# A GRU with a ternary FFN on one core: order of the first loads, the casts and warm-up products at the kernel's start

## The reference

```python
def cell(h, x):                       # 32 times, one after the other
    gi = x @ W_ih + b_ih              # [128, 256] @ [256, 768]
    gh = h @ W_hh + b_hh
    r = sigmoid(i_r + h_r)
    z = sigmoid(i_z + h_z)
    n = tanh(i_n + r * h_n)
    return (1.0 - z) * n + z * h
...
gate, up = split(hs @ ternary(w_gate_up).T)
out = x + rms_norm(silu(gate) * up) @ ternary(w_proj).T
```

## Time and profile before

| | us |
|---|---|
| median of 3 runs | 345.35 (344.94 to 345.5) |
| the profiled execution | 345.16 |
| its span, first to last instruction | 343.4 |
| TensorE busy | 338.2 (98%) |
| VectorE, ScalarE, GpSimd busy | 233.1 (68%), 224.9 (66%), 184.1 (54%) |

### The profile page before, as it was taken

How to read it: one execution, slowest core, us unless ns; L and a number is a source line. 1 busy time by engine, 2 the same in 40 slices (tenths; PEclk the granted TensorE clock), 3 DMA queues, 4 the chain that set the end, 5 groups by cost and what they waited for, 6 DMA issues and landing times.

```text
span 343.4 us, 5618 instructions
## 1 busy us (share of the span) xinstructions
PE 338.2 (98%) x2048; PEld 294.4 (86%) x2053; DVE 233.1 (68%) x462; ACT 224.9 (66%) x442; POOL 184.1 (54%) x156
## 2 busy tenths in 40 slices
PE   8999999999999999999999999999999999999996
PEld 4989988888988889888888889888888888888895
DVE  7588787999576556754678554775658555665866
ACT  6778888787755757555766666566565655756662
POOL 2316571465825536255454447454462555799694
PEclk9999999999999999999999999999999999999999
DMA  7995000054001000130001000010000100010101
GB/s 241 299 402 224 2 0 2 0 186 183 1 2 62 2 0 0 71 115 2 0 0 63 0 2 1 1 63 0 2 0 15 48 1 2 0 64 1 59 4 61
DMA packets 7891, 18.72 MB, mean 55 GB/s; under 512 B 564, under 2 KB 4788, under 8 KB 7352
## 3 DMA queue, kind: packets, MB, share of 16 engines
q1 hardware_dynamic: 7176, 17.97, 14.1%
q10 hardware_dynamic: 688, 0.39, 0.4%
HBM read 14.17 MB, written 4.19 MB: 53 GB/s over the span
## 4 chain that ended last, share of the span: by engine, by line
PE 90%; DVE 5%; issue 2%; ACT 1%; DVEq 0%
PE ps_ffn L1126 29%; PE ps_out L1164 16%; PE ps_rz L1028 6%; PE ps_rz L1033 6%; PE ps_rz L1029 6%; PE ps_n L1028 3%; PE ps_n L1033 3%; PE ps_n L1029 3%; PE ps_rz L1126 2%; PE ps_t L1119 1%; PE ps_ffn L1291 1%; PE ps_n L1077 1%; PE ps_ffn L1028 1%; PE ps_ffn L1033 1%; PE ps_ffn L1029 1%
## 5 line engine op out<-in xcount | busy, mean ns | idle before, releaser
L359 POOL TENSOR_TENSOR hid_lo<-work,hid_hi 128x512 fp32r<-128x512 f32 x62 | 81.6, 1316 | 103.5 <-ACT hid_hi L457 99.5
L1126 PE MATMUL ps_ffn<-st_hi,wguT 128*128 128x512 f32 x236 | 93.8, 397 | 0.1
L1126 PE MATMUL ps_ffn<-st_lo,wguT 128*128 128x512 f32 x236 | 92.6, 393 | 0.0
L366 POOL TENSOR_TENSOR sq_sum<-sq_sum,work 128x512 f32<-128x512 f32 x55 | 73.2, 1331 | 1.7 <-ACT work L471 0.6
L748 DVE TENSOR_TENSOR work<-work,ps_ffn 128x512 f32<-128x512 f32 x55 | 37.6, 683 | 31.4 <-ACT work L453 31.3
L457 ACT CAST hid_hi<-work 128x512 fp32r<-128x512 f32 x63 | 38.8, 616 | 23.4 <-DVE work L758 23.4
L1126 PEld LDWEIGHTS ps_ffn<-st_hi,wguT 128*128 128x128 f32 x236 | 44.4, 188 | 8.3 <-DVE work L748 0.7
L1126 PEld LDWEIGHTS ps_ffn<-st_lo,wguT 128*128 128x128 f32 x236 | 44.5, 189 | 7.3
L758 DVE TENSOR_TENSOR work<-work,ps_ffn 128x512 f32<-128x512 f32 x63 | 43.2, 686 | 4.7 <-PE ps_ffn L1126 2.8
L1164 PEld LDWEIGHTS ps_out<-wpT,hid_hi 128*128 128x128 f32 x240 | 35.8, 189 | 3.7
L1164 PE MATMUL ps_out<-wpT,hid_lo 128*128 128x256 f32 x240 | 38.8, 284 | 0.0
(11 more groups left out here) (232 smaller groups left out, 713.7 us busy)
## 6 DMA issues: line engine op xcount, KB each, us to landing
out_dram<-o_st SPq DMA_DIRECT2D x7, 512.0 KB, 2.8
xT_all<-in_x_dram SPq DMA_DIRECT2D x1, 3072.0 KB, 16.4
x_ring<-in_x_dram SPq DMA_DIRECT2D x1, 3072.0 KB, 11.2
x_ring<-in_L_ffn_w_gate_up_dram SPq DMA_DIRECT2D x4, 512.0 KB, 9.5
x_ring<-in_L_ffn_w_proj_dram SPq DMA_DIRECT2D x2, 512.0 KB, 11.7
x_ring<-in_x_dram SPq DMA_DIRECT2D x1, 1024.0 KB, 6.0
work<-in_L_cond_W_ih_dram SPq DMA_DIRECT2D x3, 256.0 KB, 4.5
work<-in_L_cond_W_hh_dram SPq DMA_DIRECT2D x3, 256.0 KB, 4.8
```

The source lines that it names most:

```text
L359: nc.gpsimd.tensor_tensor(hid_lo[:, j % RING], hid[:, j % 2], f32(hid_hi[:, j % RING]), ALU.subtract).then_inc(hid_lo_ok, 1)
L366: nc.gpsimd.tensor_tensor(sq_sum[:], sq_sum[:], hid_sq[:, j % 2], ALU.add).then_inc(sq_added, 1)
L1126: mm = pe.matmul(bank, w, group_state(part, G, k), start=(k == 0 and i == 0), stop=(k == KD - 1 and i == 1))
```

## The change

SyncE's first load is W_ih's reset piece, the transposed state cT is second; the two bias rows are issued by ScalarE behind x's step 0. ScalarE casts W_ih's reset piece before the RZ columns of the biases. GpSimd, not VectorE, makes the state's low part. VectorE splits the RZ columns after wi_lo(0). TensorE runs eight warm-up products, seeds the n bank inside first_input(0) ahead of the wi_lo products, and adds the RZ bias row inside first_state(0) ahead of the wh_lo products.

```diff
--- before.py
+++ after.py
@@ -260,12 +260,12 @@
                 for to, w, landed in ((wi, w_ih, ld_wi), (wh, w_hh, ld_wh)):
                     sp.dma_start(to[:, :, GATES[i]],
                                  w.rearrange("(k p) n -> p k n", p=P)[:, :, GATES[i]]).then_inc(landed[i], 16)
+                    if i == 0 and to is wi:
+                        sp.dma_start(cT[:], cond_t.rearrange("(k p) b -> p k b", p=P)).then_inc(ld_cT, 16)
 
             def load_inputs(first, last, landed):
                 sp.dma_start(xT_all[:, :, first:last, :], xt[:, :, first:last, :]).then_inc(landed, 16)
 
-            for i, b in enumerate((b_ih, b_hh)):
-                sp.dma_start(b_rows[:, i * G3:(i + 1) * G3], b.partition_broadcast(2)).then_inc(ld_b, 16)
             for i in range(3):
                 load_gate(i)
             load_inputs(1, 2, ld_x1)
@@ -323,6 +323,8 @@
                                         ALU.subtract).then_inc(x_lo_early, 1)
 
             input_lo(0)
+            pool.wait_ge(h_hi, 1)
+            nc.gpsimd.tensor_tensor(state(st_lo, -1), cT[:], f32(state(st_hi, -1)), ALU.subtract).then_inc(c_lo, 1)
             pool.wait_ge(wh_hi_ok, 3)
             nc.gpsimd.tensor_tensor(wh_lo[:, :, GATES[2]], wh[:, :, GATES[2]], f32(wh_hi[:, :, GATES[2]]),
                                     ALU.subtract).then_inc(wh_z_ok, 1)
@@ -540,16 +542,17 @@
 
             xt = x_t.rearrange("(k p) t b -> p k t b", p=P)
             act.dma_start(xT_all[:, :, 0:1, :], xt[:, :, 0:1, :]).then_inc(ld_x0, 16)
-            act.dma_start(cT[:], cond_t.rearrange("(k p) b -> p k b", p=P)).then_inc(ld_cT, 16)
+            for i, b in enumerate((b_ih, b_hh)):
+                act.dma_start(b_rows[:, i * G3:(i + 1) * G3], b.partition_broadcast(2)).then_inc(ld_b, 16)
             act.wait_ge(consts, 1)
             nc.scalar.activation(table[:], ones[:], ACT.Sigmoid)
             act.wait_ge(ld_x0, 16)
             input_hi(0)
             act.wait_ge(ld_b, 32)
             nc.scalar.copy(both_n(b_hi), both_n(b_all)).then_inc(b_hi_ok, 1)
+            w_ih_hi(0)
             act.wait_ge(b_sum_ok, 1)
             nc.scalar.copy(b_hi[:, RZ], b_all[:, RZ]).then_inc(b_hi_ok, 1)
-            w_ih_hi(0)
             act.wait_ge(ld_cT, 16)
             nc.scalar.copy(state(st_hi, -1), cT[:]).then_inc(h_hi, 1)
             w_hh_hi(0)
@@ -864,10 +867,6 @@
             dve.wait_ge(b_hi_ok, 1)
             nc.vector.scalar_tensor_tensor(out=both_n(b_split[0:2, :]), in0=both_n(f32(b_hi)), scalar=ident[0:2, 1:2],
                                            in1=both_n(b_all), op0=ALU.mult, op1=ALU.subtract).then_inc(b_split_ok, 1)
-            dve.wait_ge(b_hi_ok, 2)
-            nc.vector.scalar_tensor_tensor(out=b_split[0:2, RZ], in0=f32(b_hi[:, RZ]), scalar=ident[0:2, 1:2],
-                                           in1=b_all[:, RZ], op0=ALU.mult, op1=ALU.subtract).then_inc(b_split_ok, 1)
-
             def w_ih_lo(i):
                 dve.wait_ge(wi_hi_ok, i + 1)
                 cols = GATES[i]
@@ -881,8 +880,9 @@
                                         ALU.subtract).then_inc(wh_ok, 1)
 
             w_ih_lo(0)
-            dve.wait_ge(h_hi, 1)
-            nc.vector.tensor_tensor(state(st_lo, -1), cT[:], f32(state(st_hi, -1)), ALU.subtract).then_inc(c_lo, 1)
+            dve.wait_ge(b_hi_ok, 2)
+            nc.vector.scalar_tensor_tensor(out=b_split[0:2, RZ], in0=f32(b_hi[:, RZ]), scalar=ident[0:2, 1:2],
+                                           in1=b_all[:, RZ], op0=ALU.mult, op1=ALU.subtract).then_inc(b_split_ok, 1)
             w_hh_lo(0)
             w_ih_lo(1)
             w_hh_lo(1)
@@ -1301,6 +1301,9 @@
                     for k in range(KD):
                         pe.matmul(dst, part[:, 0, k, :], wi_hi[:, k, cols],
                                   start=i == 0 and k == 0 and part is xT_hi, stop=False, skip_group_check=True)
+                if i == 0:
+                    pe.wait_ge(b_split_ok, 1)
+                    seed_n(0)
                 pe.wait_ge(wi_ok, i + 1)
                 for k in range(KD):
                     pe.matmul(dst, xT_hi[:, 0, k, :], wi_lo[:, k, cols], start=False, stop=False,
@@ -1316,6 +1319,9 @@
                     for k in range(KD):
                         pe.matmul(dst, part[:, k, :], wh_hi[:, k, cols], start=False, stop=False,
                                   skip_group_check=True)
+                if i == 0:
+                    pe.wait_ge(b_split_ok, 2)
+                    bias_rows(ps_rz[:], RZ, False)
                 if i == 1:
                     seed_rz(1)
                 if i < 2:
@@ -1331,13 +1337,10 @@
                 mm.then_inc(summed, 1)
 
             pe.wait_ge(warm_ok, 1)
-            busy(10)
+            busy(8)
             pe.wait_ge(consts, 5)
             first_input(0, ps_rz[:, 0:D])
-            pe.wait_ge(b_split_ok, 2)
-            bias_rows(ps_rz[:], RZ, False)
             first_state(0, ps_rz[:, 0:D], r_sum)
-            seed_n(0)
             first_input(1, ps_n[:, 0:D])
             first_state(1, ps_n[:, D:2 * D], n_sum)
             pe.wait_ge(r_ok, 1)
```

## The result

The changed kernel takes 347.23 us (median of 5 runs, 346.64 to 347.96) against 345.35; the ratio is 1.0053, with a 95% interval of 1.0033 to 1.0074. It is 1.9 us slower, where 0.5 faster was forecast. The profiled execution took 347.96, with a span of 345.8.

The account below looks back on a forecast made before the run. TensorE, busy 90% of the span, was taken as the bound. Between z's gain of 0.6 and the state's cast's 0.55, 0.5 was taken: 344.66 from the profiled 345.16, 344.85 on the median; forecast 344.8, range 344.1 to 345.7.

Parts of the forecast that it names:

- (a): Early loads: W_ih's reset half issued 0.71 earlier, landing at 4.35 for 5.14; biases at 3.6, at worst 3.87.
- S: Start of ScalarE's cast of W_ih's reset half, wi_hi(0): 4.35, at worst 4.4 by the biases.
- (b): ScalarE's early casts: wi_hi(0) starts at 4.35; wh_hi(0) starts at 5.9 and ends at 6.5, against 6.84.
- (c): VectorE and GpSimd: the low state on GpSimd collides with VectorE's work; 0.25 charged, bounds 0 and 0.6.
- (d): TensorE's start: products begin 0.8 earlier, 0.4 gained if the clock rises at 6.65; reset sum 7.75 for 8.19.
- the clock rises later: Rival on TensorE's start: each microsecond more at 1.2 GHz costs half a microsecond; 346.5 if near 10; chance 0.07.
- (e): Late next: ScalarE's q_abs(0), awaiting the gate-up load at 12.15, lets the state's cast come 0.55 earlier; 0.5 taken.
- it doesn't do what it says: Rival on the early loads: W_ih's half lands no earlier than 5.14, TensorE only idles, 345.35; chance 0.07.

Follow-up runs that it names:

- e10: The kernel before without the work on the split biases (bias rows added as zeros): 345.71 us, ratio 1.0009.
- e8: The kernel before with the biases on ScalarE's queue behind x and the state first on SyncE, W_ih's reset half second: 347.41 us, ratio 1.0057.
- e7: The kernel before with one load moved, W_ih's reset half ahead of the two bias rows on SyncE: 347.52 us, ratio 1.0059.
- e3: The kernel before with the new order of loads alone, ten warm-ups: 347.84 us, ratio 1.0071.
- e9: The changed kernel (eight warm-ups, its loads) without the work on the split biases, bias rows added as zeros: 344.82 us, ratio 0.9984.
- e1: The changed kernel with ten warm-up products instead of eight: 346.72 us, ratio 1.0041.
- e6: The changed kernel with ten warm-ups and the state's low part back on VectorE: 346.24 us, ratio 1.0030.
- e12: The changed kernel with the loads of before, ten warm-ups and the state's low part on VectorE: 345.34 us, ratio 1.0002.
- e2: The kernel before with eight warm-up products instead of ten, nothing else changed: 345.56 us, ratio 1.0014.
- e4: The changed kernel with the load order of before, eight warm-ups: 346.78 us, ratio 1.0039.
- e5: The kernel before with one edit, GpSimd making the state's low part: 345.53 us, ratio 1.0006.
- e13: The kernel before with x first on SyncE, W_ih's reset half second, state third, biases alone on ScalarE's queue, ten warm-ups: 345.67 us, ratio 1.0015.
- e14: The same loads as e13 on the kernel before, with nine warm-ups: 346.42 us, ratio 1.0032.

## Why the prediction was wrong

**The step that failed is (a), its sentences on x and the biases.** The price of x's landing was left at what the row of before had. The only delay that x's cast was given was ScalarE's third issue, 0.2. But that 2.4 was the time of a load that had the DMA engines almost alone: SyncE issued 12 KB beside it, and W_ih's half only 0.7 later. Issued together with 256 KB it took 3.6. The biases behind it on the same queue were expected at 3.6, at worst 3.87, by the state's 2.3; they landed at 4.85, and it is this that sets S in (b). 0.3 of it is issuing: the second bias row was issued at 1.87, not 1.57. The rest is the landing, and the "worst" end was no worst. The state's 2.3 is the lowest of six traces with the loads of before, which go up to 4.3 (e10). The Trainium skill, page "DMA: Bandwidth & Descriptors", section "Queues, rings and completion order", states that each DMA engine takes packets in turn from the queues that have work. By that rule x on one queue and W_ih on the other would take turns. That x gets later with the size of the load beside it (e8, e7, e3) agrees; even turns from the start the trace does not show. The DMA queues from 2.5 to 3.0 (packets, MB, share of 16 engines; q1 is SyncE's, q10 ScalarE's), changed kernel, then before:

```profile
q1 hardware_dynamic: 126, 0.13, 73.6%
q10 hardware_dynamic: 39, 0.02, 13.2%
```

```profile
q10 hardware_dynamic: 260, 0.12, 83.9%
q1 hardware_dynamic: 21, 0.02, 42.7%
```

In the changed kernel ScalarE's queue moved nothing before 2.5 and little before 3.0, while W_ih went first; x's 128 KB came mostly from 3.0 to 3.75. In the kernel before x and the state together had nearly all of their packets by 3.0. Why W_ih goes first, with both loads issued within 0.01, stays open. The prediction cited the section on shared engines for the size of the prize, and did not turn it on the load that would have to share.

**(a), the rest.** W_ih's half took 3.4 for the 3.7 used, and later loads came 0.66 to 0.9 earlier where 0.22 to 0.5 was said. The gain sought was there; the kernel could not take it. The third issue cost more than its 0.2: ScalarE's table load stands at 2.14 for 1.72. Behind the late x that did not show.

**(b)** S was to be 4.35, with "at worst 4.4 by the biases". It was 5.37. The queue on ScalarE is in order, and x's and the biases' casts stand ahead of W_ih's. The cover for that was the other way round: W_ih's late landing had hidden the bias work (e10), and loading W_ih first removed the cover (e9: 2.4 us with what hangs on it in clock and outside the span).

**(c)** The collision was right as a mechanism and too small. The charge was 0.25, less than the prediction's own rows give: GpSimd's 0.74 from 6.4 and then wh_lo(0)'s 0.69 end at 7.83, not 7.5. The RZ split took 1.21 for 0.73, 0.48 more, and a second collision, of the bias sum with GpSimd's xT_lo (1.25, or 1.01 in e1, for 0.68), was not foreseen: the late biases bring the two together. Undone in e6, the first is worth 0.13 inside the span: the low state on VectorE takes that time itself. It was not the main cause. The Trainium skill's rule (page "SBUF — State Buffer", section "Who interferes with whom") agrees with the traces in what collides and nearly in size: the RZ split, at 7.29 behind wi_lo(0), takes 0.48 longer while GpSimd works from 7.13 to 7.96. Waiting out the whole instruction it would have ended at 8.69; it ended at 8.50.

**(d)** The walk on TensorE used a rise of the clock at 6.65 as if it were a property of the kernel. It is one draw: the first products ran at the high level at 5.39 in e9, at 5.88 in e12, and at the low one up to 10.3 in e2. The rival "the clock rises later" had the right sign and place, a wait of TensorE behind eight warm-ups, and got 7%. Its price of half a microsecond for each microsecond is near e2's trace, where a rise some 4 us later put the state's cast back by 1.64. In the changed kernel's trace it is not a late rise, though, but a fall after a first rise (8.3 to 11.64), which no row of before could show. It was judged by the wait that followed from S = 4.35, 0.3 at most, and the wait was 1.09.

**(e)** q_abs(0) was not late next: its load was 0.9 earlier, and nothing came early enough to wait for it. What was predicted for the later steps held: the shift at the first state is that of step 8 and of the end.

The loss then reads: 1.1 inside the span from late x and biases (e1's trace; 0.13 of it goes with GpSimd's low state), about 0.5 at the median from the clock (the changed kernel against e1), 0.35 outside the span. That is about the 1.9 measured. The parts do not simply add: e4, with the loads of before and eight warm-ups, still loses 1.35 by its ratio, 0.35 of it outside the span. The rival "it doesn't do what it says" asked whether W_ih would be early; it should have asked what would be late for it.

## What to carry to other kernels

When a load is moved to the front, price the loads that it will now run beside, not only itself: a time to landing read from a trace holds for the traffic of that trace. List what each in-order engine handles ahead of the new arrival, since work that was free behind a slow load becomes the path once that load is fast. Cutting warm-up products has no fixed price here: the executions of e2, e4 and the changed kernel spread over 1.3 to 3.6 us. So judge it by many executions; one trace shows one draw, of the clock and of a load's landing alike.

## What the runs showed of the hardware that I had not expected

- The granted clock in the rows reads 1.00 also where TensorE works at 1.2 GHz at the start (warm-ups 0.427 apart, e2's first products 0.43 a pair up to 10.27). In these traces it shows 0.50 only for a fall after a first rise. The spacing of the products is the surer reading.
- The idle time depends on the clock too. Ten warm-ups took 4.45 in e1, e5 and e13, but 4.13, 4.04, 3.83 and 3.70 in e6, e3, e7 and e12, where the level rose during them; they then end up to 0.7 earlier.
- The clock fell with idle times of 1.09 (changed kernel), 2.06 (e3) and 2.07 (e7) ahead of the first product, whatever the number of warm-ups. Executions lay within 0.3 us with 0.32 and 0.47 of idle in the profile (e1, e6) and spread over 2.2 to 3.6 with 0.82 and 0.52 (e2, e4). e10 with 0.92 and e12 with 0.72 spread over 1.5, and so did e13 with 0.15. The kernel before, with none in its trace, stands at 344.7 to 346.3 but for 5 of the 99 executions beside e1 to e14, between 347.1 and 347.6. No single figure divides them.
- One more GpSimd operation made every execution 0.35 longer outside the span (e5, and e1 and e4 against e6 and e12), while e9, which has it too but fewer operations elsewhere, did not. What this time is stays open.
- The time to landing of one early load differs between executions with the same loads: 2.3 to 4.3 for the state and 3.3 to 4.2 for W_ih's reset half over the six traces with the loads of before.
- With W_ih and x issued at once, the first data came later, not only slower. The stretch from 2.0 to 2.5, changed kernel, then before:

```profile
2.00:2.50 0.50, 0.50 (x3) 0.15 (x2) 0.32 (x2) 0.36 (x1) 0.39 (x2) 1.00 0.36 74
```

```profile
2.00:2.50 0.50, 0.50 (x3) 0.15 (x1) 0.32 (x2) 0.50 (x1) 0.39 (x3) 1.00 0.80 241
```
